# M and N built head by head and mixed by a block-diagonal product through DRAM; twelve shared groups before the experts, their gelu one step ahead

## The reference

```python
sin_table = sin(num_value[:, None] / 1000 * freqs)          # freqs 1..128
h = where(is_num[:, None], sin_table, weight)[x]            # 12500 rows of 128
a = layernorm(h)                                            # 128 sequences of 128 tokens
q, k, v = a @ Wq, a @ Wk, a @ Wv                            # H = 8 heads of DH = 64
dots = where(eye, -1e-9, q k^T * scale[head])
dots = einsum('bhij,hg->bgij', dots, mix_pre)
attn = einsum('bhij,hg->bgij', softmax(dots), mix_post)
h = h + (attn v) @ Wout + bout
x2 = layernorm(h)
y = gelu(x2 @ Ws1 + bs1) @ Ws2 + bs2                        # shared FFN, 512 wide
for bank in (sp, fq):                                       # top-1 of 8 experts, capacity 1280
    y = y + gate * keep * (gelu(x2 @ W1[e] + b1[e]) @ W2[e] + b2[e])
out = h + y
```

## Time and profile before

| | us |
|---|---|
| median of 3 runs (1503.89 to 1504.49) | 1504.01 |
| the profiled execution's own time | 1516.0 |
| its span in the trace | 1514.3 |
| PE busy, share of the span | 1465.3, 97% |
| ACT busy | 1146.8, 76% |
| DVE busy | 1047.0, 69% |
| POOL busy | 959.1, 63% |

### The profile page before, as it was taken

How to read it: one execution, slowest core, us unless ns; L and a number is a source line. 1 busy time by engine, 2 the same in 40 slices (tenths; PEclk the granted TensorE clock), 3 DMA queues, 4 the chain that set the end, 5 groups by cost and what they waited for, 6 DMA issues and landing times. The chain is left out here.

```text
span 1514.3 us, 33889 instructions
## 1 busy us (share of the span) xinstructions
PE 1465.3 (97%) x11160; PEld 1339.9 (88%) x11160; DVE 1047.0 (69%) x2811; ACT 1146.8 (76%) x3477; POOL 959.1 (63%) x991
## 2 busy tenths in 40 slices
PE   5789999999999999999999999988999999999999
PEld 2469888888888988889888898877999999999999
DVE  7887788788777887778887787763344333356665
ACT  5589888888888888888888888865555555555555
POOL 7175567888788888788878877664677566510000
PEclk9999999999999999999999999999999999999999
DMA  7324511211211111111111111022244234456665
GB/s 237 132 73 163 164 38 49 69 48 42 60 38 39 55 42 36 35 56 34 36 56 34 37 38 48 26 60 67 69 116 106 70 71 109 120 158 190 189 184 146
DMA packets 171503, 126.48 MB, mean 84 GB/s; under 512 B 30309, under 2 KB 154959, under 8 KB 171330
## 3 DMA queue, kind: packets, MB, share of 16 engines
q1 hardware_dynamic: 153794, 104.15, 23.3%
q0 software_dynamic: 17536, 20.17, 4.8%
HBM read 61.64 MB, written 78.66 MB: 93 GB/s over the span
## 5 line engine op out<-in xcount | busy, mean ns | idle before, releaser
L1129 ACT ACTIVATE expd<-masked,nmax 128x128 f32<-128x128 f32 x1024 | 396.0, 393 | 0.3 <-DVE nmax L1282 0.3
L925 POOL TENSOR_TENSOR prob<-expd,rtotal 128x1024 f32<-128x1024 f32 x128 | 243.5, 1902 | 117.3 <-DVE rtotal L1251 115.8
L1265 DVE COPY_PREDICATED masked<-off_diag,ps_s 128x1024 f32<-128x1024 int32 x128 | 175.0, 1367 | 164.3 <-PE ps_s L1018 164.3
L1062 PE MATMUL ps_o<-u,probT 128*128 128x128 f32 x2048 | 249.0, 275 | 0.0
L1062 PEld LDWEIGHTS ps_o<-u,probT 128*128 128x128 f32 x2048 | 238.9, 191 | 0.0
L1129 ACT ACTIVATION_READ_ACCUMULATOR expd<-masked,nmax 128x1 f32 x1024 | 197.0, 192 | 0.0
L1138 ACT ACTIVATE u<-ps_ut 128x1024 f32<-128x1024 f32 x128 | 131.4, 1026 | 66.3 <-PE ps_ut L1073 66.3
L1227 DVE TENSOR_TENSOR w_lo<-ps_w,w_hi 128x512 fp32r<-128x512 f32 x256 | 164.3, 681 | 0.9 <-ACT w_hi L1167 0.9
L1167 ACT ACTIVATE w_hi<-ps_w 128x512 fp32r<-128x512 f32 x256 | 146.1, 595 | 15.7 <-PE ps_w L1048 9.3
L1158 ACT ACTIVATE probT<-ps_ut 128x1024 f32<-128x1024 f32 x128 | 131.4, 1027 | 33.9 <-PE ps_ut L1030 27.5
L1046 PE MATMUL ps_w<-xT_hi,M_hi 128*128 128x256 f32 x512 | 154.1, 301 | 3.0 <-DVE xT_lo L1221 2.2
(11 more groups left out here) (261 smaller groups left out, 3824.9 us busy)
## 6 DMA issues: line engine op xcount, KB each, us to landing
turned<-x2T SPq DMA_DIRECT2D x32, 256.0 KB, 2.2
answers_sp<-zeros SPq DMA_DIRECT2D x16, 512.0 KB, 4.3
answers_fq<-zeros SPq DMA_DIRECT2D x16, 512.0 KB, 3.8
xT<-turned SPq DMA_DIRECT2D x56, 128.0 KB, 2.3
sh_back<-answers_sp SPq DMA_DIRECT2D x56, 128.0 KB, 2.4
sh_back<-answers_fq SPq DMA_DIRECT2D x56, 128.0 KB, 2.5
out<-res SPq DMA_DIRECT2D x56, 128.0 KB, 2.1
h_sb<-in_L_tok_weight SPq DMA_DIRECT2D x12, 512.0 KB, 5.9
```

What stands on the lines that cost most here:

```text
L925: nc.gpsimd.tensor_tensor(prob[k % 2][:, :].rearrange("p (g j) -> p g j", g=H), expd[k % 2][:, :].rearrange("p (g j) -> p g j", g=H), rtot ...
L1062: mm = nc.tensor.matmul(ps_o[:, 0:D], probT[k % 2][:, g * N:(g + 1) * N], u[k % 2][:, g * D:(g + 1) * D], start=(g == 0), stop=(g == H - 1))
L1129: ins = nc.scalar.activation(expd[(k - 1) % 2][:, g * N:(g + 1) * N], masked[(k - 1) % 2][:, g * N:(g + 1) * N], ACT.Exp, bias=nmax[(k - 1 ...
L1265: nc.vector.copy_predicated(masked[k % 2][:, :].rearrange("p (g j) -> p g j", g=H), off_diag[:, :].unsqueeze(1).to_broadcast([P, H, N]), p ...
```

## The change

**Setup.** PE multiplies the weights head by head first (`by_heads`, eight matmuls of 64 rows and 128 columns for M and eight for N), ACT copies the product out (`cut`), SP writes it to DRAM and reads it back with heads laid over partitions (`heads_out`, `heads_in`), PE mixes the heads by two matmuls with a 128 x 128 block-diagonal matrix (`by_bands`, `mixer`), ACT copies again, SP takes it through DRAM back (`mix_out`, `mix_in`), ACT makes M_hi and N_hi (`high`), POOL M_lo and N_lo. The eight POOL products are gone. Beside that: the chain for the frequencies (`turn_b`) goes from DVE to POOL; the thousandths of the numbers are made in one pass of 98 columns; `kept` is written ahead of the weights' loads; the gathers of the first tiles' numbers go ahead of those of their rows; the two fills of `masked` go from ACT to POOL; `WARM` is 6.

**Head.** `HEAD` is 12. Each group's transposed rows come from `turned`, a DRAM buffer that attention writes anyway, by a load of 128 KB (`load_head`) instead of normalising and transposing; the first layer's result alternates between `ps_s` and `ps_w`; a step of PE is down(n-2), then up(n), so the gelu of a group has the up of the next one ahead of its own down.

**Shared FFN.** 52 groups are left; the head's rows are added by group of 256 rows, one every second step, twelve of them.

The core of the diff, cut:

```diff
-HEAD = 8
+HEAD = 12
-WARM = 13
+WARM = 6
...
-            for c in range(2 * HC):
-                mix(c)
...
+            for w in range(2):
+                link.inc(nc.gpsimd.tensor_tensor(mixer[:, w, :].rearrange("p (a h) -> p a h", h=H), bands[:, :, :],
+                                        co[:, w, :].unsqueeze(1).to_broadcast([P, P // H, H]), ALU.mult))
+            for k in range(2):
+                link.inc(nc.gpsimd.tensor_copy(masked[k][:, :].rearrange("p (g j) -> p g j", g=H),
+                                               diag[:, :].unsqueeze(2).to_broadcast([P, H, N])))
...
+            def heads_out(w):
+                sp.wait_ge(S["cut"], w + 1)
+                sp.dma_start(by_head[w], whole_sb[:, w, :]).then_inc(S["mix_put"], 16)
+            def heads_in(w):
+                sp.wait_ge(S["mix_put"], 16 * (w + 1))
+                sp.dma_start(parted[:, w, :].rearrange("p (b j) -> p b j", b=H), bands_of(by_head[w])).then_inc(s_mix[w], 16)
+            def mix_out(w):
+                sp.wait_ge(S["cut"], w + 3)
+                sp.dma_start(bands_of(by_mix[w]), whole_sb[:, w, :].rearrange("p (b j) -> p b j", b=H)).then_inc(S["mix_put"], 16)
+            def mix_in(w):
+                sp.wait_ge(S["mix_put"], 16 * (w + 3))
+                sp.dma_start(parted[:, w, :], by_mix[w]).then_inc(s_mix[w], 16)
...
+                if c in (5, 7, 10, 11):
+                    cut((5, 7, 10, 11).index(c))
+                if c == CHUNKS - 1:
+                    high(0)
...
+            high(1)
...
+            def by_bands(w):
+                pe.wait_ge(S["made"], made[f"mixer{w}"])
+                pe.wait_ge(s_mix[w], 16)
+                pe.wait_ge(S["cut"], w + 2)
+                for half in range(2):
+                    at = slice(half * 512, (half + 1) * 512)
+                    ins = nc.tensor.matmul(ps_m[:, at], mixer[:, w, :], parted[:, w, at], start=True, stop=True)
+                ins.then_inc(S["M"], 1)
...
+        STEPS_PE = {129: (0,), 130: (1,), 131: (2,), 132: (3,), 135: (4,), 136: (5,), 137: (6,), 139: range(7, HEAD + 2)}
...
+            def load_head(groups):
+                for n in groups:
+                    need(sp, S["head_xlo"], n - 3)
+                    sp.dma_start(head_x(n), turned[n // 2, :, n % 2 * GROUP:(n % 2 + 1) * GROUP]).then_inc(s_head[n % 4], 16)
...
+            def head_steps(k):
+                for n in STEPS_PE.get(k, ()):
+                    if n >= 2:
+                        head_down(n - 2)
+                    if n < HEAD:
+                        head_up(n)
...
-        HEADS_FROM = 4
+        HEADS_FROM = 1
-            return (n, n) if (k - HEADS_FROM) % 3 == 0 and 0 <= n < 2 * HEAD else None
+            return n if (k - HEADS_FROM) % 2 == 0 and 0 <= n < HEAD else None
```

More of the change, by code:

```diff
@@ L331, in setup, with bands_of @@
         ps_c = pb("ps_c", 512)
-        names = ("made", "num", "isn", "ids0", "numbers", "kept", "small", "freq", "numbers0", "rows0", "stat0", "early_put", "num_f", "numT", "numT_out", "angle", "whole", "reduced", "turn", "sine", "done", "put",
-                 "weights", "wT", "wT_out", "coef", "coefd", "coef_out", "mixed", "M", "hi")
+        names = ("made", "num", "isn", "ids0", "numbers", "kept", "small", "freq", "numbers0", "rows0", "early_put", "num_f", "numT", "numT_out", "angle", "whole", "reduced", "link", "sine", "done", "put",
+                 "weights", "wT", "wT_out", "coef", "coefd", "coef_out", "M", "cut", "mix_put")
         S = {n: sem("s_" + n) for n in names}
         s_row = [sem(f"s_row{k}") for k in range(4)]
+        s_mix = [sem(f"s_mix{k}") for k in range(2)]
+        by_head = [nc.dram_tensor(f"by_head{w}", (P, H * D), F32).ap() for w in range(2)]
+        by_mix = [nc.dram_tensor(f"by_mix{w}", (P, H * D), F32).ap() for w in range(2)]
+        def bands_of(t):
+            return t.rearrange("(b a) (h j) -> (a h) b j", a=P // H, h=H)
         w_main = weight[0:P * VR, :].rearrange("(p r) d -> p (r d)", p=P)
@@ L651, in halves @@
-                link.wait()
-                for part in (0, 2):
-                    ins = nc.vector.tensor_tensor(num_hl[:, chunks, 0:n, part + 1], src, num_hl[:, chunks, 0:n, part].bitcast(F32), ALU.subtract)
-                ins.then_inc(S["num_f"], 1)
+                src = part[:, 0, chunks.start * VC:chunks.start * VC + (chunks.stop - chunks.start) * n].rearrange("p (c r) -> p c r", r=n)
+                high, low = (num_hl[:, chunks, 0:n, k:PARTS:2] for k in range(2))
+                both = src.unsqueeze(3).to_broadcast([P, chunks.stop - chunks.start, n, 2])
@@ L717, in _ @@
                     for t in range(OWN):
-                        ins = nc.vector.bn_aggr(C.mv1[0][:, t, :], C.stat0[:, t, :])
-                    ins.then_inc(S["stat0"], 1)
-            for half, src in enumerate((ps_t, ps_c)):
-                at = slice(half * 512, (half + 1) * 512)
-                dve.wait_ge(S["hi"], 2 + half)
-                link.inc(nc.vector.tensor_tensor(mats["N_lo"][:, at], src[:, :], mats["N_hi"][:, at].bitcast(F32), ALU.subtract))
+                        link.inc(nc.vector.bn_aggr(C.mv1[0][:, t, :], C.stat0[:, t, :]))
+                    link.wait()
             link.wait()
@@ L803, in attention @@
         s_late = sem("a_late_put")
+        s_head = [sem(f"a_head_x{k}") for k in range(4)]
         FETCHED_AT = {-2: range(OWN, 8), 2: (8, 9, 10), 3: (11,), 4: (12, 13, 14)}
@@ L1189, in step @@
                         for f in range(FC):
-                            ins = nc.scalar.activation(hidden(masked[m % 2], f), hidden(ps_s, f), ACT.Gelu, bias=bs1_c[:, f:f + 1])
+                            ins = nc.scalar.activation(hidden(masked[m % 2], f), up(m, f), ACT.Gelu, bias=bs1_c[:, f:f + 1])
                         ins.then_inc(S["head_gelu"], 1)
```

375 lines of the change are left out of this document (191 added, 184 removed).

## The result

The changed kernel takes 1515.09 us (median of 20 runs, 1512.5 to 1518.07), the kernel before 1507.12 in the runs beside it: a ratio of 1.0043 (95% interval 1.0024 to 1.0063). It is slower, where 1496.7 was forecast, and outside the range of 1488 to 1503.

A forecast was written before the change was run, and what follows sets the result against it. PE was taken as the bound, busy 1465.3 of 1514.3 us. Head and last stage -6.5 and setup -0.8 gave -7.3: 1516.0 to 1508.7, less 12.0 for the profiled execution, 1496.7; eight-in-ten range 1488 to 1503.

The forecast's parts named there:

- It stood 12.0 above the median of 1504.01, and I take the difference over whole: Whole kernel: the profiled execution's 12.0 us above the median was subtracted unchanged, taking 1508.7 to 1496.7.
- Setup, "58 to 61.5 ... I take the late end": Setup: stall of 14.3 us goes, transfer chain comes; N_lo ends at 61.5 instead of 63.8, -2.3 us.
- The rival with SP's queue: Setup: hops, loads and puts share one ordered queue, so setup ends at 75.7; +7 us, 1511; chance 0.06.
- Clock at the start of attention, +1.5: Start of attention: PE at its lower clock, twelve to eighteen matmuls cost 0.1 us more each; +1.5, bounds 0 and +4.
- The drain, 5.0 of 5.77 filled: Drain at the head: 5.0 of PE's 5.77 us idle filled by the new step order, 0.8 staying.
- The last stage, 0 for the twelve groups: Last stage: twelve added groups of 256 rows cost 0 as DVE's waiting covers them; without that cover, 16 us.
- The head as a whole, -6.5: Head and last stage: -12.6 + 13.2 - 2.1 - 5.0 = -6.5 us; bounds -7.3 and -1.5.
- The rule of the two engines: Setup: DVE with two SBUF inputs and POOL reading SBUF exclude each other; N_lo could delay puts, setup's sum +1.2, not -0.8.

The follow-up runs named there:

- short runs: Kernel before, unchanged: those of its 20 runs between 1503.4 and 1507.3 us, 12 of them, median 1504.2; the other 8 have median 1516.6.
- long execution: Kernel before, unchanged: the profiled execution that the prediction read, with DVE's put of sines at 15.58 us; it took 1516.0 us.
- the part alone: Kernel before with only the new head and last stage, setup as before: 1497.24 us, ratio 0.9935.
- with gaps: Kernel before with POOL's first gather held until DVE's third reduction and a wait between POOL's eight products: 1507.0 us.
- the short execution of before: Kernel before, unchanged, profiled again in the follow-up: DVE's put took 1.63 us and attention started at 53.74; it took 1504.92 us.

## Why the prediction was wrong, step by step

- **"It stood 12.0 above the median of 1504.01, and I take the difference over whole": failed.** The 12.0 were no offset of the profile but, for 10.4 of them, the very stall that the prediction read in the earlier trace rows. The short runs have no such stall, so the removal of it had nothing to give against 1504. Three runs within 0.6 us and a profiled one 12 above them were the hint that I had.
- **Setup, "58 to 61.5 ... I take the late end": mis-sized.** The end went from 63.8 to 69.2, +5.4 instead of -2.3. N_lo ends 7.7 after the 61.5, and the steps of the prediction's chain show where. N is mixed from 50.9 on instead of 43 to 45, 6 late: the row of 3.1 for a transfer came from puts that the stall had spread out, and with loads, hops and puts close together a first hop takes 11.3 for 7 to 9, behind cuts that are 1 to 1.6 late themselves. From there to the cut of N it is 6.8 instead of 3 to 4, as PE's mixing, for which the sum has no term, takes 3.75. The second hop and the split were as summed or shorter, 8.0 (for 6.9 to 8.3) and 3.5 (for 4.4). The run without the first pair of hops agrees with the first of these, by 5.7. Against the short group's setup the loss is 69.62 - 53.74 = 15.9, of which the four hops' transfers are 8.6.
- **The rival with SP's queue** had the right side, 1511 by a setup end of 75.7. Its mechanism was half right: it is less the order of the queue than the transfers it fills the engines with, since moving hops ahead in it brought the read 2.6 forward and the kernel nothing.
- **Clock at the start of attention, +1.5: right.** The first POOL product of attention comes 6.7 later than in the long execution, 1.2 more than the 5.4 by which setup ends later.
- **The drain, 5.0 of 5.77 filled: right.** 5.05 were. From the same matmul to PE's last down it is 49.33 for 43.73, +5.6, forecast as 13.2 - 2.1 - 5.0 = 6.1.
- **The last stage, 0 for the twelve groups: nearly.** The steps are 3.16 (results at 1391.39 and 1394.55). But PE waits 1.8 once, before the first layer of the fourth group, where it did not wait before. It waits for a piece of DVE's list, in which the first group's sums stand ahead, and these wait for their loads:

```profile
1342.85 0.36 PE L1814 MATMUL sh_ps_h<-sh_xT_hi,w_hi 128*128 128x256 f32 x1 [1.78 <-PEq L1526]
...
1350.47 0.61 DVE L1863 SCALAR_TENSOR_TENSOR sh_part<-sh_back,gates,h_sb 128x128 f32<-128x128 f32 x2 [3.63 <-DMA sh_back<-answers_fq]
...
1352.18 0.60 DVE L1884 SCALAR_TENSOR_TENSOR sh_one_part<-sh_one_back,gates,h_sb 128x128 f32<-128x128 f32 x2
...
1353.18 0.38 PE L1814 MATMUL sh_ps_h<-sh_xT_hi,w_hi 128*128 128x256 f32 x1 [1.82 <-DVE sh_xT_lo L1855]
```

and before:

```profile
1333.03 0.35 PE L1760 MATMUL sh_ps_h<-sh_xT_hi,w_hi 128*128 128x256 f32 x1 [1.78 <-PEq L1475]
...
1339.47 0.61 DVE L1809 SCALAR_TENSOR_TENSOR sh_part<-sh_back,gates,h_sb 128x128 f32<-128x128 f32 x2 [2.42 <-DMA sh_back<-answers_fq]
```

The first group's loads were issued ahead of those of the head's group (1346.97 and 1347.48), which then ran beside them, and DVE could start 7.62 after the stage's first matmul instead of 6.44; the head's sums (L1884) took 0.5 more ahead of PE's piece. With the head's groups five steps in, 0.8 of the wait went.

- **The head as a whole, -6.5: right,** -7.2 by the part alone, but in part by luck. In the profiles the drain is +5.6 and the last stage -11.1 (170.2 for 181.3, from PE's first matmul there to the span's end), together -5.5; the experts between them, which no edit touches, were 2.2 shorter. Such lengths vary from profile to profile without an edit: from POOL's last product of attention to its last indirect write of the experts it is 327.0 to 330.0 in three executions with the old head.
- **The rule of the two engines.** A put beside POOL's products takes 15.6 in three executions, 2.63 with gaps and 1.63 in the short one. The Trainium skill (SBUF — State Buffer, "Who interferes with whom") lets the second of two such instructions wait for the first; the runs agree for one product, and show besides that the wait can last through eight. The price that the prediction worked out by the rule, +1.2, should be +1.1 (-0.8 + 1.9). No put waited for N_lo; one waited beside POOL's mixer and fills, costed at 0, in the profile with thirteen warming matmuls (3.57).

## What to carry to other kernels

When a profiled execution and the plain runs differ by far more than the plain runs among themselves, find the stage in which they differ before a sum is made from the profile: a stall that stands in the trace may be absent from the runs it is to be subtracted from, and the rows beside it are shaped by it. A stall between two engines that shut each other out can hang on a start some tenths of a microsecond earlier; look what decides who comes first, and move that (here two small copies) before replacing the work. A price of a transfer is that of the traffic around it: sum the bytes of the stretch, not the rows of a quieter one.

## What was not expected of the hardware

DVE's copy waited through all eight back-to-back products of POOL (15.57) when it came 0.44 us after the first had started, and no longer than 1.7 us in an execution in which the first product had itself waited for DVE. With a semaphore wait between the products it waited 1.3. And the granted clock reads 1.00 in setup, before and after, while a pair of 512-column angles takes 1.22 us in one place of it and 0.73 in another, and the mixing 3.75 or 1.88 by whether PE was filled:

```profile
25.36 1.22 PE L566 MATMUL ps_a<-freq,numT 32*128 32x512 f32 x2
...
30.16 0.73 PE L566 MATMUL ps_a<-freq,numT 32*128 32x512 f32 x2
```

(both in the short execution of before). In the first 5.4 us of the changed kernel's attention it reads 1.00 too, with matmuls of 256 columns at 0.41. Later the row does fall: in the kernel before it reads 0.60 from 87 to 90 us, where the same matmuls take 0.41, and 1.00 from 90 on. So the prediction read its 0.93 rightly, as a mean over both levels; the 1.00 of setup, beside it, says nothing of the level there, and only the durations do.
